# A Mamba-style mixer's input products: from one pair of PSUM banks to two pairs in turn

## What is computed

```
proj = layernorm(x) @ in_proj_w.T          # 512 -> 8192 (gate) + 8192 (x) + 1024 (B) + 1024 (C) + 128 (dt)
gate, xBC, dt = split(proj)
xBC = silu(causal_conv4(xBC) + conv_b)     # 4 taps along time, one filter per channel
x, B, C = split(xBC)                       # heads 16g to 16g+15 share B and C of group g
y = scan of (x, B, C, softplus(dt), A) + D * x
g = y * silu(gate)
out = (g * rsqrt(mean(g*g over a group) + eps) * norm_w) @ out_w.T
```

## Time and profile before

| | us |
|---|---|
| median of 3 runs (lowest to highest) | 2008.33 (2005.29 to 2013.21) |
| the profiled execution, its time | 2012.99 |
| its span, first to last instruction | 2011.3 |
| TensorE busy (share of span) | 1869.6 (93%) |
| its weight loads | 1482.2 (74%) |
| GpSimd | 1406.6 (70%) |
| VectorE | 1389.6 (69%) |
| ScalarE | 1172.5 (58%) |
| mean granted clock of TensorE, of 1 | 0.948 |

### The profile page before, as it was taken

How to read it: one execution, slowest core, us unless ns; L and a number is a source line. 1 busy time by engine, 2 the same in 40 slices (tenths; PEclk the granted TensorE clock), 3 DMA queues, 4 the chain that set the end, 5 groups by cost and what they waited for, 6 DMA issues and landing times. The chain is left out here.

```text
span 2011.3 us, 32277 instructions
## 1 busy us (share of the span) xinstructions
PE 1869.6 (93%) x10572; PEld 1482.2 (74%) x10572; DVE 1389.6 (69%) x1799; ACT 1172.5 (58%) x2109; POOL 1406.6 (70%) x1413
## 2 busy tenths in 40 slices
PE   6989998766999999999999999999999999999967
PEld 4855776545788778778878887887888788877855
DVE  5547455567676787677768766876777687668756
ACT  3221332334776667576757766775767577667723
POOL 4000422443899699789969996997899699969844
PEclk9966798877999999999999999999999999999978
DMA  3000000103343334243323433342433234323301
GB/s 106 1 1 4 19 2 1 32 27 116 109 130 106 95 95 126 75 123 114 115 86 110 126 105 96 95 129 73 126 110 116 86 115 122 105 95 100 115 17 57
DMA packets 174834, 170.14 MB, mean 85 GB/s; under 512 B 11072, under 2 KB 142272, under 8 KB 174656
## 3 DMA queue, kind: packets, MB, share of 16 engines
q1 hardware_dynamic: 173696, 167.84, 27.3%
q10 hardware_dynamic: 960, 0.05, 0.0%
HBM read 165.22 MB, written 2.62 MB: 83 GB/s over the span
## 5 line engine op out<-in xcount | busy, mean ns | idle before, releaser
L143 PE MATMUL ps<-mix_xnT_hi,mix_w_hi 128*128 128x512 f32 x1152 | 463.8, 403 | 12.1 <-DVE mix_xT L1536 6.2
L145 PE MATMUL ps<-mix_xnT_hi,mix_w_lo 128*128 128x512 f32 x1152 | 455.9, 396 | 0.0
L144 PE MATMUL ps<-mix_xnT_lo,mix_w_hi 128*128 128x512 f32 x1152 | 455.6, 395 | 0.0
L1536 DVE SCALAR_TENSOR_TENSOR mix_xT<-ps,mix_cur,mix_xT 128x510 f32<-128x510 f32 x378 | 279.7, 745 | 139.3 <-ACT mix_xT L1403 130.4
L1354 POOL TENSOR_SCALAR_AFFINE_SELECT mix_spread<-mix_spread 128x256 f32<-128x256 f32 x512 | 308.9, 638 | 0.0
L1556 DVE TENSOR_TENSOR mix_decay<-mix_decay,mix_cb 128x1536 f32<-128x1536 f32 x128 | 303.3, 2407 | 4.5 <-ACT mix_decay L1429 4.5
L143 PEld LDWEIGHTS ps<-mix_xnT_hi,mix_w_hi 128*128 128x128 f32 x1152 | 217.9, 189 | 68.3 <-issue 12.5
L1452 ACT ACTIVATE mix_g_hi<-mix_gated 128x512 fp32r<-128x512 f32 x128 | 81.0, 633 | 316.8 <-POOL mix_gated L1331 284.7
L1427 ACT ACTIVATE mix_decay<-mix_spread,mix_cur_ncum 128x256 f32<-128x256 f32 x512 | 253.6, 495 | 12.9 <-DVE mix_cur_ncum L1608 12.9
L145 PEld LDWEIGHTS ps<-mix_xnT_hi,mix_w_lo 128*128 128x128 f32 x1152 | 217.7, 189 | 51.0
L144 PEld LDWEIGHTS ps<-mix_xnT_lo,mix_w_hi 128*128 128x128 f32 x1152 | 218.1, 189 | 47.3
(11 more groups left out here) (261 smaller groups left out, 3525.2 us busy)
## 6 DMA issues: line engine op xcount, KB each, us to landing
mix_spread<-cum_rows SPq DMA_DIRECT2D x128, 512.0 KB, 3.8
mix_w_raw<-in_w_in_stream SPq DMA_DIRECT2D x144, 256.0 KB, 4.9
mix_spread<-cum_rows SPq DMA_DIRECT2D x128, 256.0 KB, 4.8
mix_wo_raw<-in_w_out_T SPq DMA_DIRECT2D x64, 256.0 KB, 4.9
att_w_raw<-in_w_attn_T SPq DMA_DIRECT2D x12, 256.0 KB, 2.7
x<-in_x SPq DMA_DIRECT2D x8, 256.0 KB, 4.6
ffn_w_raw<-in_w_ffn_T SPq DMA_DIRECT2D x2, 1024.0 KB, 6.2
out_rows<-x SPq DMA_DIRECT2D x8, 256.0 KB, 2.0
```

What stands on the lines that cost most here:

```text
L143: pe.matmul(out, lh, rh, start=(k == 0), stop=False)
L144: pe.matmul(out, lh, rl, start=False, stop=False)
L145: last = pe.matmul(out, ll, rh, start=False, stop=(k == tiles - 1))
L1536: dve.scalar_tensor_tensor(out=d[:, :, shift:T], in0=src[:, :, 0:T - shift], scalar=w[:, MK - 1 - shift:MK - shift], in1=d[:, :, shift:T], ...
```

## The change

The products alternate between two pairs of banks by their place in `NEXT`: x and B write banks 0 and 1, the gate and C banks 2 and 3. The readers of the gate and of C are given those banks. In TensorE's program the single "reader before" becomes a list of two, so that a product waits for the reader of the product two before, which used the same banks: x for the taps of the x before it, the gate for the silu of the gate before it, B for the last x, C for the last gate, and the next group's first x and gate for B's and C's taps. In the lead-in, product 3 (x of pair 0) waits for B's taps as before, and product 4 (the gate of pair 0) for C's taps and no longer for those of product 3. The instructions of every engine and their order are the same.

```diff
+        def bank_of(item):
+            return 2 * (NEXT.index(item) % 2)
...
             def silu_gate(n_prod, dst):
                 for half in range(2):
                     act.wait_ge(projected, 2 * (n_prod - 1) + half + 1)
-                    act.activation(dst[:, half * 512:(half + 1) * 512], ps[:, half, :], ACT.Silu).then_inc(silu_g, 1)
+                    act.activation(dst[:, half * 512:(half + 1) * 512], ps[:, 2 + half, :], ACT.Silu).then_inc(silu_g, 1)
...
-                            tap0(n_product(g, (kind, 0)), dst, w, bias, half)
+                            tap0(n_product(g, (kind, 0)), dst, w, bias, half, bank_of((kind, 0)))
...
-                            conv_taps(n_conv(g, (kind, 0)), dst, cur_w((kind, 0)), half)
+                            conv_taps(n_conv(g, (kind, 0)), dst, cur_w((kind, 0)), half, bank_of((kind, 0)))
...
-            before = [(None, 0)]
+            readers = [("conv", 0), ("conv", 1)]
 
-            def product(n, at):
+            def product(n, at, reader):
                 pe.wait_ge(w_lo_done, n)
+                kind, count = readers.pop(0)
+                readers.append(reader)
                 for half in range(2):
-                    kind, count = before[0]
                     if kind == "conv":
                         pe.wait_ge(convolved, 6 * count + 3 * half + 3)
-                    elif kind == "gate":
+                    else:
                         pe.wait_ge(silu_g, 2 * count + half + 1)
                     cols = slice(half * 512, (half + 1) * 512)
-                    three_pass(pe, ps[:, half, :], lambda k: (w_hi[:, at % 2, k, :], w_lo[:, at % 2, k, :]),
+                    three_pass(pe, ps[:, 2 * ((at + 1) % 2) + half, :],
+                               lambda k: (w_hi[:, at % 2, k, :], w_lo[:, at % 2, k, :]),
                                lambda k: (xnT_hi[:, k, cols], xnT_lo[:, k, cols])).then_inc(projected, 1)
...
                 if not first:
-                    before[0] = ("conv", n_conv(g - 1, CONVS[-1]))
+                    readers[:] = [("conv", n_conv(g - 1, item)) for item in CONVS[-2:]]
...
-            before[0] = ("conv", 0)
-            product(3, 3)
-            before[0] = ("conv", 2)
-            product(4, 4)
-            before[0] = ("gate", 0)
+            product(3, 3, ("conv", 2))
+            product(4, 4, ("gate", 0))
```

More of the change, by code:

```diff
@@ L1669, in _ @@
         def _(pe):
-            before = [(None, 0)]
-            def product(n, at):
+            readers = [("conv", 0), ("conv", 1)]
+            def product(n, at, reader):
                 pe.wait_ge(w_lo_done, n)
+                kind, count = readers.pop(0)
+                readers.append(reader)
                 for half in range(2):
-                    kind, count = before[0]
                     if kind == "conv":
                         pe.wait_ge(convolved, 6 * count + 3 * half + 3)
-                    elif kind == "gate":
+                    else:
                         pe.wait_ge(silu_g, 2 * count + half + 1)
                     cols = slice(half * 512, (half + 1) * 512)
-                    three_pass(pe, ps[:, half, :], lambda k: (w_hi[:, at % 2, k, :], w_lo[:, at % 2, k, :]),
+                    three_pass(pe, ps[:, 2 * ((at + 1) % 2) + half, :],
+                               lambda k: (w_hi[:, at % 2, k, :], w_lo[:, at % 2, k, :]),
                                lambda k: (xnT_hi[:, k, cols], xnT_lo[:, k, cols])).then_inc(projected, 1)
             def next_product(g, item):
-                product(n_product(g, item), LEAD + NEXT.index(item))
-                before[0] = ("gate", n_gate(g, item[1])) if item[0] == "g" else ("conv", n_conv(g, item))
+                product(n_product(g, item), LEAD + NEXT.index(item),
+                        ("gate", n_gate(g, item[1])) if item[0] == "g" else ("conv", n_conv(g, item)))
             def turn_x(uses, conv, buf):
```

## The result

The changed kernel takes 2005.7 us, the median of 22 executions (1998.88 to 2010.76); the kernel before, over 22 executions beside it, 2009.78 (2005.29 to 2017.33). The ratio is 0.9977 with a 95% interval of 0.9968 to 0.9986: 4.6 us less, 2.8 to 6.4 (4.1 by the medians). The forecast of 2005.2, 3.1 less, holds. The forecast held so small a difference to be beyond what a measurement tells; with 22 executions of each it is told, as the interval leaves out 1. In one execution of a kernel further down, heads_and_end_busy, the granted clock was 0.554 and the time 3076 us, and its ratio is that of the other nine.

A forecast was written before the change was run, and what follows sets the result against it. TensorE's product stream was taken as the bound, so only its waits for PSUM banks could come back. 3.3 + 1.4 − 1.6 = 3.1 us less, from 2008.33 to 2005.2 us; range 1999.0 to 2011.5.

The forecast's parts named there:

- the rival that TensorE is not full: Bank waits fill the time TensorE's weight loads are not busy; half of it back gives 1865 us; chance 0.02.
- (a): The x product no longer waits for the gate's two reads; 0 in the steady part.
- (b): The gate's product no longer waits for the taps of the x just before it; 3.3 us gained.
- (c): C's product no longer waits for B's taps; 0 gained.
- (d): Four stalls at the mixer's start, where TensorE is not yet full; 1.4 us gained in all.
- the first stall: Ahead of the gate's first product at the mixer's start; on the path, gain 1.4 us, between 0 and 1.42.
- The second and third: Stalls ahead of group 0's g1 and g2; gain 0, as y of pairs 0 and 1 waits for VectorE.
- (e): Half clock at the start, after idle time ahead of y of pair 1; 1.6 us lost, bounds 0 and 6.4.
- The signs of being wrong: VectorE's decay or GpSimd's split in TensorE's steady-part waits, half clock outside the mixer's ends, or slower taps or silus.

The follow-up runs named there:

- heads_and_end_busy: heads_busy with 20 more matmuls of 512 columns ahead of the last pair's y; median 2003.47 us, ratio to before 0.9964.
- start_only: The kernel before, with only product 4 (the first gate) in the other pair of banks; median 2007.31 us, ratio to before 0.9986.
- c_in_first_pair: The changed kernel with C's product and its readers back in banks 0 and 1; median 2007.94 us, ratio to before 0.9984.
- kept_busy: The changed kernel with twelve unread matmuls in each of the first two waits ahead of y; median 2001.16 us, ratio to before 0.9954.
- heads_busy: kept_busy with VectorE's four C·B copies together, and four unread matmuls ahead of C·B and of pair 0's y in groups 1 to 7; 2003.87 us.

## Why the prediction was right

- **What bounds the kernel.** TensorE's product stream, as the even starts said. The changed kernel keeps 20.56 us a pair, and the rival that TensorE is not full (by the load busy time, now 960.22 of 1200) is out: with the waits on the taps gone TensorE's busy time in the window changed by 2.76 us, and the steady part got 2.6 to 5.5 us shorter.
- **(a), x's wait on the gate: 0.** Right; start_only and c_in_first_pair leave nothing for it.
- **(b), the gate's wait on the taps: 3.3 taken, 4.7 measured.** The mechanism and the place were right, and 3.25 of it lie there. Mis-sized were the smaller cases, for which 0.4 was added: the step from pair 1 to 2 gave 1.47. They also used up what y had to spare: the prediction left it 0.3 us behind the decay, and it starts 0.06 behind it, held by VectorE in pair 3 of every group. That costs about 0.02 us in most groups and 0.2 in group 1 (20.58 and 20.78 for 20.56), so there is nothing left to spare at this place.
- **(c), C's wait on B's taps: 0 taken, about 1 measured.** The pause at the head of a group (4.0 us in five places) had no named releaser in the list and was passed over. With C back in the first banks it is there (3.9 us in five places); with C in the others 2.7 us are left, ahead of C·B. What the engine waited for in it stays open.
- **(d), the first stall: 1.4 taken, 1.5 at y of pair 0 in the change, 1.7 alone. The second and third: 0**, right; the waits ahead of y grew to 3.61 and 3.15 us, with 3.1 and 4 forecast.
- **(e), the clock in the start: one stretch, 1.6, taken.** Two came, one on each y. Their price is y of pair 2 in the changed kernel against kept_busy, 2.35 us. With them the start is 0.6 us slower than before, where the forecast had 0.2.
- **Not in the sum:** the clock in the heads, 3.0 us in the first profile and none in the second. The range took it in by luck, not by a term: the long window's 1.00 did not tell that a single head can fall.
- **The signs of being wrong.** Two of the three that the prediction named came without making it wrong: the decay in TensorE's list in the steady part, at the small price above, and half clock outside the mixer's ends, in the first profile. The third did not: taps and silus are as fast as before.

So 4.6 + 0.9 from the steady part, less 0.6 to 0.8 in the start and up to 3 for the heads, gives 2.0 for the mixer in the first profile and 4.7 in the second, around the forecast's 3.1; the two measurements by the ratio say 4.6 and 2.4. That the sum came so near is in part luck: (b) and (c) were taken some 2.4 too small together, and the clock was taken too cheap, by 0.75 in the start and by up to 3 in the heads.

Of the clock: the trace shows it at half rate in the start (1.13 us a group of y for 0.66) and in two heads, and that took back 2.35 and 3.0 us. The Trainium skill ("TensorE: Matmul & The Clock Gate", A second HAM failure mode: psum-queue depth-cycling) reports a clock that swings with small idle times between groups of matmuls, in a kernel that cycles through banks. The trace shows no swing from bank to bank; it agrees in the start only, where the clock fell at y behind waits of 3.61 and 3.15 us and stayed up with the waits filled. Of the heads no run shows that their stretches come with the change (2 and 0 of 7 in its two profiles), and in heads_busy the clock fell with no gap longer than 0.18 us.

## What to carry to other kernels

Count a wait as gain only up to the next wait on the path: the banks removed all of TensorE's waits on the taps; the two large ones in the start, which were not on the path, came back ahead of y. On an engine whose clock answers to its work, ask also where the removed idle time gathers; filling it with matmuls that nobody reads gave 2.4 us, half of the 4.7 that the change gives the mixer where no head falls to half rate. Measure with marks inside the trace when an effect is no larger than the spread of the medians, and take more than one profile of a kernel.

## What the runs showed of the hardware

- The granted clock fell behind 16 matmuls of one column each in 1.84 us, with no gap of TensorE longer than 0.18 us in that head (heads_busy). Matmuls of 512 columns in the place of 3.6 and 3.2 us of waiting kept it at 1.00 (kept_busy).
- The same kernel at the same place, once with half rate and once without: 2 heads of 7 in one profile, 0 of 7 in the other.
